# Layer 0 of a gated cross-attention kernel: stacks of two heads with the mask's rows in the contraction, loaded from DRAM, and row maxima taken bank by bank

## What is computed

```python
# layer 0: 16 heads of width 8; x is (16, 56, 128), ctx is (16, 1500, 128)
v = einsum('nlhd,od->nlho', ctx heads, Wv); k = ... Wk; q = einsum('nqhd,od->nqho', layernorm(x) heads, Wq)
energy = einsum('nqhd,nkhd->nhqk', q, k)
energy = where(mask == 0, -1e20, energy)              # mask: (16, 1, 56, 1500), all ones in the inputs
attn = softmax(energy / sqrt(128), axis=3)
x = x + tanh(g_xattn[0]) * (einsum('nhqk,nkhd->nqhd', attn, v).reshape(...) @ Wo.T + bo)
# then a routed feed-forward block (layer 0), attention with 16 heads of width 64 and a quantised block (layer 1)
```

## Time and profile before

| | us |
|---|---|
| median of 3 runs | 1247.57 |
| profiled execution | 1247.09 |
| its span, first to last instruction | 1245.3 |
| layer 0's attention, first row scores to the last block | 50 to 493 |
| TensorE busy over the span | 1132.1 |
| VectorE, ScalarE, GpSimd busy | 885.6, 699.6, 516.7 |
| mean granted TensorE clock | 0.972 |

### The profile page before, as it was taken

The page is one execution under the profiler, slowest core; times in us unless marked ns, Lnnn a source line. Parts: engine busy times, 40 slices in busy tenths (PEclk is TensorE's granted clock), DMA queues, the critical chain, the costliest instruction groups (busy, mean ns, idle before and its releaser), DMA issues.

```text
span 1245.3 us, 27942 instructions
## 1 busy us (share of the span) xinstructions
PE 1132.1 (91%) x10056; PEld 646.7 (52%) x10056; DVE 885.6 (71%) x1242; ACT 699.6 (56%) x967; POOL 516.7 (41%) x352
## 2 busy tenths in 40 slices
PE   4789999999999989778878999999999999999984
PEld 2255656566565646523434555555555555555542
DVE  7766666666666664587787868768676867867668
ACT  2345555555555536445566656666565656666542
POOL 8546666676666744332212322322232223223210
PEclk9899999999999989799998999999999999999996
DMA  3456565455554462000006776667575775667530
GB/s 106 123 169 199 167 182 156 150 156 159 179 157 151 133 157 66 1 1 26 1 13 131 145 143 135 144 136 151 123 145 117 147 149 126 147 133 150 112 63 15
DMA packets 222263, 151.29 MB, mean 121 GB/s; under 512 B 184576, under 2 KB 195312, under 8 KB 222208
## 3 DMA queue, kind: packets, MB, share of 16 engines
q1 hardware_dynamic: 221920, 150.56, 50.1%
q10 hardware_dynamic: 288, 0.00, 0.0%
HBM read 62.23 MB, written 25.39 MB: 70 GB/s over the span
## 4 chain that ended last, share of the span: by engine, by line
PE 75%; DVE 10%; issue 7%; ACT 6%; SPq 1%; DMA 1%; POOL 0%; ACTq 0%; DVEq 0%; POOLq 0%
PE bank L879 17%; PE bank L897 16%; PE bank L754 7%; PE bank L847 6%; PE bank L778 5%; PE bank L782 5%; PE bank L795 4%; DVE region L1701 2%; PE bank L855 2%; PE bank L919 2%; ACT region L1227 2%; PE bank L1120 2%; DVE e_row L1519 2%; PE bank L1082 1%; PE bank L825 1%
## 5 line engine op out<-in xcount | busy, mean ns | idle before, releaser
L1519 DVE CUSTOM_DVE_ANT_0 e_row<-bank,region 112x1500 f32<-112x1500 f32 x128 | 220.1, 1720 | 125.4 <-PE bank L754 124.1
L1227 ACT ACTIVATE region<-bank 125x896 f32<-125x896 f32 x192 | 176.0, 917 | 203.2 <-PE bank L782 203.2
L1558 DVE TENSOR_REDUCE neg_max<-bank 128x1 f32<-128x1500 f32 x112 | 192.7, 1721 | 130.7 <-PE bank L879 130.7
L879 PE MATMUL bank<-region 128*128 128x500 f16 x1008 | 235.1, 379 | 3.2 <-ACT e_row L1254 1.8
L1263 ACT COPY region<-bank 128x768 f16<-128x768 f16 x224 | 178.0, 794 | 88.2 <-PE bank L847 88.2
L1254 ACT ACTIVATE e_row<-bank,neg_shift 128x1500 f32<-128x1500 f32 x112 | 169.3, 1511 | 68.8 <-DVE neg_shift L1562 38.6
L573 POOL CAST u_w<-e_row 128x1500 f16<-128x1500 f32 x56 | 80.7, 1442 | 215.2 <-ACT e_row L1254 215.2
L573 POOL CAST wg_sb<-e_row 128x1500 f16<-128x1500 f32 x56 | 82.0, 1464 | 198.5 <-ACT e_row L1254 154.4
L879 PEld LDWEIGHTS bank<-region 128*128 (+1 forms) x1008 | 97.2, 98 | 107.9 <-issue 3.4
L778 PE MATMUL bank<-row_of,region 112*128 112x448 bf16 x384 | 137.7, 359 | 7.6 <-ACT region L1227 7.6
L782 PE MATMUL bank<-region 97*128 (+1 forms) x768 | 137.6, 260 | 0.0
(11 more groups left out here) (218 smaller groups left out, 1518.3 us busy)
## 6 DMA issues: line engine op xcount, KB each, us to landing
region<-region SPq DMA_DIRECT2D x192, 96.0 KB, 2.2
turned_rows<-region SPq DMA_DIRECT2D x16, 768.0 KB, 3.8
region<-turned_rows SPq DMA_DIRECT2D x32, 384.0 KB, 3.5
c_in<-in_ctx SPq DMA_DIRECT2D x16, 750.0 KB
split_rows<-region SPq DMA_DIRECT2D x16, 750.0 KB
region<-in_mask_Bx1xSxS_if SPq DMA_DIRECT2D x32, 328.1 KB
region<-split_rows SPq DMA_DIRECT2D x24, 250.0 KB
g_w<-split_rows SPq DMA_DIRECT2D x24, 250.0 KB
```

Of the source, the lines that this page charges most:

```text
L879: last = pe.matmul(score_banks1(par, t)[:, k, :], q1[:, ql, b, 128 * t:128 * (t + 1)], c_t1[par][:, cl, 4 * k:4 * k + 4, 0:KP], start=(ql ...
L1227: act.activation(p0[:, 2 * i:2 * i + 2, :], ring0("s", h, i)[0:KP, :, 0:HALF_ROWS], ACT.Exp, scale=SCALE0)\
L1519: dve.tensor_tensor_reduce(out=masked.rearrange("p (a k) -> p a k", a=3), in0=bank[0:R0, 0:3, 0:4 * KP], in1=mask_bias[par][:].rearrange(" ...
L1558: dve.tensor_reduce(neg_max[:, t:t + 1], score_banks1(par, t), AX.XY, ALU.max, negate=True)\
```

## The change

Layer 0 is rewritten as follows.

- **Stack.** A stack now holds two heads (one tile): rows 0 to 15 the high part, 16 to 31 the low, 32 the maximum, 33 to 48 the high again, and 49 to 104 the mask's 56 rows. There are 8 of them in a batch (HP), so KS = 105 rows.
- **Loads.** The stacks of batch b + 1 are loaded in `layer0(b)` in two halves of four. Each half has three DMAs from `turned_rows` in DRAM (16 rows x 4 stacks x 3 KB) and one that repeats the mask's rows four times (56 rows x 4 x 3 KB, within SBUF). They wait until `turned_out` of that batch has landed. Splitting, turning and storing are done two batches ahead, the transposes in h = 1 at i = 1 and 3.
- **Transposed scores.** A chunk is four matmuls of 112 columns with the four stacks; the mask's own matmul is gone.
- **Row maxima.** Each of a tile's three banks is reduced by itself, and each of its three matmuls waits for the reduction of that bank one tile earlier. One more small reduction a half combines them. The mask is in the scores already.
- **Places.** `c_split0` and `c_t0` move into the buffers of `g_w` and `u_w`; these weights are now loaded in batch 14 and both scaled by GpSimd in batch 15. The mask is read once in a batch, not twice. The preparation of q0 (64 rows instead of 96) is shorter by a few VectorE instructions.

```diff
 # places
-        c_stack = [carve([97, G, KC, 128], F16) for _ in range(2)]
+        c_stack = [carve([KS, HP, KC, 128], F16) for _ in range(2)]
-        c_split0 = carve([128, KC, 2, G, 32], F16)
-        c_t0 = carve([128, 2, KC, 128], F16)
+        c_split0, c_t0 = (w[:].rearrange("p e i -> p (e i)")[:, 0:KC * 128].bitcast(F16) for w in (g_w, u_w))
...
 # order of the PSUM pairs
-        RING0 = [("s", 0, 0), ("prep", 0), ("s", 0, 1), ("spread", 0), ("s", 0, 2), ("prep", 1), ("s", 0, 3), ("s", 0, 4),
-                 ("s", 0, 5), ("neg", 0), ("s", 1, 0), ("s", 1, 1), ("spread", 1), ("s", 1, 2), ("s", 1, 3), ("s", 1, 4),
-                 ("s", 1, 5), ("neg", 1)]
+        RING0 = [("s", 0, 0), ("s", 0, 1), ("spread", 0), ("s", 0, 2), ("s", 0, 3), ("s", 0, 4), ("s", 0, 5), ("neg", 0),
+                 ("s", 1, 0), ("s", 1, 1), ("prep", 0), ("spread", 1), ("s", 1, 2), ("s", 1, 3), ("prep", 1),
+                 ("s", 1, 4), ("s", 1, 5), ("neg", 1)]
...
         def sync_stack(sp, b, par):
             wait_apart(sp, "sp", (sem("st0"), (b - 1) * (2 * NP)))
-            for n in range(2):
-                wait_apart(sp, "sp", (sem(f"ct_done0_{n}"), b + 1))
-                for g in range(G):
-                    for at in ((0, 64), (32,))[n]:
-                        sp.dma_start(c_stack[par][at:at + 32, g], c_t0[32 * g:32 * g + 32, n])\
-                            .then_inc(sem(f"stack{par}_{g}"), 16)
+            wait_apart(sp, "sp", (sem("turned_out0"), 16 * (b + 1)))
+            wait_apart(sp, "sp", (sem("mask_done"), b + 1))
+            for half in range(2):
+                pairs = slice(4 * half, 4 * half + 4)
+                turned = turned_rows[b].rearrange("(g p) n c k -> p n g (c k)", p=2 * D0)
+                for at, n in ((0, 0), (2 * D0, 1), (33, 0)):
+                    sp.dma_start(c_stack[par][at:at + 2 * D0, pairs].rearrange("p g c k -> p g (c k)"), turned[:, n, pairs])\
+                        .then_inc(sem(f"stack{par}_{half}"), 16)
+                sp.dma_start(c_stack[par][KS - S:KS, pairs], mask_rows[par].unsqueeze(1).broadcast_to((S, 4, KC, 128)))\
+                    .then_inc(sem(f"stack{par}_{half}"), 16)
...
 # SyncE, a batch
             def layer0(b, par, first, last):
+                ahead = B - b if isinstance(b, int) else B
+                if ahead > 1:
+                    sync_stack(sp, b + 1, 1 - par)
+                if ahead > 3:
+                    sync_load_mask(sp, b + 3)
+                if ahead > 2:
+                    sync_split_out(sp, b + 2)
+                    sync_turned_out(sp, b + 2)
+                if ahead > 3:
+                    sync_load_context(sp, b + 3, 1 - par)
...
 # GpSimd, a batch
             def layer0(b, par, first, last):
-                if not last:
-                    mask0(b + 1, 1 - par)
+                if not (isinstance(b, int) and b + 2 >= B):
+                    mask0(b + 2, par)
+                    split0(b + 2, par)
...
-                if isinstance(b, int) and b >= B - 2:
+                if last:
                     pool.wait_ge(sem("in_ffn0"), 16 * 5)
-                    w = (g_w, u_w)[b - (B - 2)]
-                    pool.tensor_scalar(w[:], w[:], W_SCALE, None, ALU.mult).then_inc(sem("gu_scaled"), 1)
+                    for w in (g_w, u_w):
+                        pool.tensor_scalar(w[:], w[:], W_SCALE, None, ALU.mult).then_inc(sem("gu_scaled"), 1)
...
         def pe_rows0(pe, b, par, t):
-            if t % 2 == 0:
-                pe.wait_ge(sem(f"stack{par}_{t // 2}"), per_use(b, par, 48))
-            wait(pe, sem("max_done0"), b * T0 + t)
+            if t % 4 == 0:
+                pe.wait_ge(sem(f"stack{par}_{t // 4}"), per_use(b, par, 64))
             for k in range(3):
-                last = pe.matmul(bank[:, k, 0:4 * KP], q0_flat[0:96, bass.ds(b * ROWS + R0 * t, 128)],
-                                 c_stack[par][0:96, t // 2, 4 * k:4 * k + 4, 0:KP], start=True, stop=True)
-            last.then_inc(sem("scores0"), 1)
+                wait(pe, sem("bank_max0"), 3 * (b * T0 + t - 1) + k + 1)
+                pe.matmul(bank[:, k, 0:4 * KP], q0_flat[0:KS, bass.ds(b * ROWS + R0 * t, 128)],
+                          c_stack[par][0:KS, t, 4 * k:4 * k + 4, 0:KP], start=True, stop=True).then_inc(sem("scores0"), 1)
...
 # pe_st0
             for n in range(2):
                 c = 2 * i + n
-                into = ring0("s", h, i)[:, n, :]
-                pe.matmul(into[:, 0:HALF_ROWS], mask_flat[par][:, KP * c:KP * c + 128], row_of[:].rearrange("p h s -> p (h s)"),
-                          start=True, stop=False)
-                for g in range(2):
-                    rows = HALF_ROWS * h + GC * g
-                    last = pe.matmul(into[:, GC * g:GC * (g + 1)], c_stack[par][0:97, 2 * h + g, c, :],
-                                     q0[0:97, b, rows:rows + GC], start=False, stop=(g == 1))
+                for g in range(4):
+                    rows = HALF_ROWS * h + R0 * g
+                    last = pe.matmul(ring0("s", h, i)[:, n, R0 * g:R0 * (g + 1)], c_stack[par][0:KS, 4 * h + g, c, :],
+                                     q0[0:KS, b, rows:rows + R0], start=True, stop=True)
             last.then_inc(sem("st0"), 1)
...
         def dve_max0(dve, b, par, t):
-            if t == 0:
-                dve.wait_ge(sem("mask_done"), b + 1)
-            wait_apart(dve, "dve", (sem("scores0"), b * T0 + t + 1))
-            dve.tensor_tensor_reduce(out=masked.rearrange("p (a k) -> p a k", a=3),
-                                     in0=bank[0:R0, 0:3, 0:4 * KP],
-                                     in1=mask_bias[par][:].rearrange("p (a c) k -> p a (c k)", a=3),
-                                     scale=-1.0, scalar=3.0e38, op0=ALU.add, op1=ALU.min,
-                                     accum_out=neg_max[0:R0, t:t + 1]).then_inc(sem("max_done0"), 1)
+            for k in range(3):
+                dve.wait_ge(sem("scores0"), 3 * (b * T0 + t) + (k + 1))
+                dve.tensor_reduce(bank_max[0:R0, t, k:k + 1], bank[0:R0, k, 0:4 * KP], AX.X, ALU.max)\
+                    .then_inc(sem("bank_max0"), 1)
```

More of the change, by code:

```diff
@@ L517, in _ @@
             sync_split_out(sp, 0)
+            sync_turned_out(sp, 0)
             sync_stack(sp, 0, 0)
-            sync_turned_out(sp, 0)
             sync_load_mask(sp, 1)
-            batches(sp, layer0)
+            sync_split_out(sp, 1)
+            sync_load_context(sp, 2, 0)
+            sync_load_mask(sp, 2)
+            sync_turned_out(sp, 1)
+            layer0(0, 0, True, False)
+            layer0(1, 1, False, False)
+            with sp.Fori(1, LAST - 1) as i:
+                layer0(i * 2, 0, False, False)
+                layer0(i * 2 + 1, 1, False, False)
+            for b in range(B - 4, B):
+                layer0(b, b % 2, False, b == B - 1)
             sp.wait_ge(sem("split_out0"), 16 * B)
@@ L629, in mask0 @@
             def mask0(b, par):
-                wait_apart(pool, "pool", (sem("mask_in"), (b + 1) * 32), (sem("max_done0"), (b - 1) * T0),
-                           (sem("st0"), (b - 1) * (2 * NP)))
-                pool.tensor_scalar(mask_bias[par][:], mask_in[:].rearrange("q (p c) -> q c p", c=KC),
-                                   0.0, NEG, ALU.is_equal, ALU.mult).then_inc(sem("mask_done"), 1)
+                wait_apart(pool, "pool", (sem("mask_in"), 16 * (b + 1)))
+                if not (isinstance(b, int) and b < 2):
+                    for half in range(2):
+                        wait_apart(pool, "pool", (sem(f"stack{par}_{half}"), per_use(b - 2, par, 64)))
+                pool.tensor_scalar(mask_rows[par][:, :, 0:KP], mask_in.rearrange("q (p c) -> q c p", c=KC),
+                                   0.0, -MASK_ROW, ALU.is_equal, ALU.mult).then_inc(sem("mask_done"), 1)
             def context_pv0(b, par):
@@ L963, in layer0 @@
                                 pe_rows0(pe, after[0], after[1], 4 * after[2] + 2)
-                            if h == 0 and not last:
-                                wait_ring0(pe, b, par, "prep", 1)
-                                pe_prep0(pe, b + 1, 1, ring0("prep", 1))
                     if has_after:
@@ L1277, in act_context0 @@
                 act.wait_ge(sem("turned_out0"), 16 * b)
-                for g in range(G):
-                    act.wait_ge(sem(f"stack{1 - par}_{g}"), per_use(b - 1, 1 - par, 48))
             act.copy(c_t0[:, n].rearrange("p c k -> p (c k)"),
@@ L1312, in layer0 @@
                         act_exp0(act, b, par, h, i)
-                        if h == 0 and i in (0, 2) and not last:
-                            act_context0(act, b + 1, 1 - par, i // 2, ring0("prep", i // 2))
+                        if h == 1 and i in (1, 3) and not (isinstance(b, int) and b + 2 >= B):
+                            act_context0(act, b + 2, par, i // 2, ring0("prep", i // 2))
                         if h == 0 and i == 1 and par == 1 and not (isinstance(b, int) and b < 3):
```

(2 more changed lines are left out.)

163 lines of the change are left out of this document (81 added, 82 removed).

## The result

The changed kernel takes 1405.28 us (median of 4 runs, 1403.69 to 1406.92) against 1248.09: 1.126 times as long, interval 1.123 to 1.128. Slower was forecast, but by 37 us, not 157, and 1405 lies outside the stated range and above every rival. The profiled execution took 1403.69 us.

A forecast was written before the change was run, and what follows sets the result against it. The DMA queue, through five engines, was taken to bound the changed kernel at 29.0 us a batch instead of 26.1: +47 by batch 13, -14 for the last batches, +4 tail, total +37, 1285 us; 8-in-10 range 1198 to 1312.

The forecast's parts named there:

- The stall of about 5.6 us a batch: TensorE's wait for the stack before tile 0's row scores; about 5.6 us a batch, not shortening the DMA queue.
- a sum over five engines, 29.0 us: DMA queue per batch: 15.3 us without stacks, 9.8 for 16-row transfers, 3.9 for the mask; 29.0 us together.
- The clock: TensorE's clock may fall to 1.2 GHz after each stall; counted as nothing.
- rival 3: DMA queue with mask copies at 6.6 us: 31.7 us a batch, 1317 us; shares chance 0.60 with the forecast.
- TensorE's saving: Transposed scores: four 112-column matmuls start 0.05 us apart, a chunk takes 0.20 for 0.38 us, saving 4.3 us a batch.
- Rival 4: Transposed scores: small matmuls cost more than 0.05 us, at most 0.093; 1250 us with stacks hidden; chance 0.03.
- the 23.4 worked out: Engines alone, without the DMA queue: 21.8 + 1.0 + 0.6 = 23.4 us a batch.
- VectorE: Row maxima: a 500-column reduction takes 0.68 us, three about 1.85; VectorE's batch 19.5 us, under TensorE's 21.8.
- Start: First batches: second half of batch 0 starts at about 86 instead of 77 us, that of batch 1 12 us late.
- Tail: End of layer 0: ScalarE's first split casts wait for both weight scalings, one behind the other in batch 15; +4 us.
- All three DMA rivals: DMA queue per batch: stacks hidden 22.1 us, in between 26.8 us, worse than forecast 31.7 us.
- the hidden one: Stack loads stay hidden, 16-row transfers at the engines' rate: queue 22.1 us a batch, total 1197 us; chance 0.22.

The follow-up runs named there:

- Kernel 1: Changed kernel with the context's load issued ahead of the turned context's store: 1355.99 us, ratio 1.084.
- 7: Changed kernel with transposes in h = 0, GpSimd's split ahead of its mask, each stack half loaded after its last reader: 1486.57 us.
- Kernel 5: Changed kernel with the 125-row context load and split context store each moved as 112 and 13 rows: 1291.67 us, ratio 1.032.
- Kernel 10: Changed kernel with stacks loaded for batches 0 and 1 only, GpSimd's mask behind the second division in two instructions, its load behind the context's: 1221.96 us.
- kernel 3: Changed kernel with stacks loaded for batches 0 and 1 only: 1249.97 us, ratio 1.002.
- kernel 6: Changed kernel with the context's load ahead of the turned context's store, and 125 rows moved as 112 and 13: 1274.65 us, ratio 1.019.
- kernel 9: Changed kernel; 112 and 13 rows, transposes in h = 0, stack halves loaded behind context and mask, GpSimd's mask in two pieces, scaling by expert: 1242.25 us.
- kernel 12: Kernel before the change with maxima bank by bank, 112 and 13 rows, and weights' scaling by expert: 1234.15 us, ratio 0.989.

## Why the prediction was wrong

**The step that failed** is "The stall of about 5.6 us a batch doesn't shorten the queue: the next split goes out when its context has come in, the next turned context after it, and the stack behind both", and with it the batch as a sum over five engines, 29.0 us. It took the queue as always full and TensorE as what waits for it. But the queue waits for TensorE too: stack, h = 1, transposes, store, stack. What counts is the sum of latencies around that loop, 37.3 us. Kernels 1 and 7 change the order of the work alone, not a byte and not an engine, and give 33.7 and 43.9 us a batch for 37.3, which no sum of bytes per engine explains. Kernel 5 takes the load off the five, and still waits for its stacks. The parts were all to be seen: the order of the issues in the diff, TensorE's half of 12.4 us, and the context's load ahead of the stack. I even wrote the chain down for the start, and not for the steady part.

**The clock: a term put at nothing.** The prediction says of TensorE's lower level "it has the slack, so I count nothing". But TensorE's half with the transposes is a term of the loop. Kernel 10 has the same stretch, from the row scores to the turned context's store, without a stall before it:

```profile
254.95:265.65 10.70, 10.03 (x174) 6.68 (x174) 7.96 (x13) 6.67 (x8) 10.46 (x9) 1.00 0.19 72
```

10.7 us at a granted clock of 1.00, against 13.1 at 0.78 in the changed kernel, whose clock is at 0.50 (1.2 GHz) for the first 5.4 us behind the wait. That is 2.4 us a turn, some 31 of the 144 us.

**Sizes.** By the packets in the trace the queue is in flight 34 of 37.3 us, not 29. The context's load holds the five engines 13 us beside the stack's writes, where I took the 5.9 of the earlier trace rows; what they have of the stack and mask behind it takes 11, not 13.7; nothing is in flight for 3.3, not 0. The rate to 16 rows was right, the one to the mask's was not. Kernel 1's queue with stack alone, then with mask rows alone:

```profile
317.00:321.00 4.00, 0.92 (x16) 0.59 (x12) 1.39 (x4) 1.35 (x3) 4.00 (x4) 1.00 1.05 128
321.50:324.50 3.00, 0.00 (x0) 0.00 (x0) 0.00 (x0) 0.00 (x0) 1.90 (x3) 0.50 1.01 208
```

128 GB/s to 16 rows (forecast 120), 208 to the mask's 56, whose upper bound of 6.6 us holds and not the 3.9 that I took. With these rates the five engines' sum is 15.3 + 9.2 + 6.6 = 31.1 us, close to rival 3's 31.7, and still 6 short of the batch. The Trainium skill (SBUF — State Buffer, Door 1: The DMA port swizzle) gives 109 for four ports; the trace has a sixth more, in a window in which three transfers to different groups of 16 rows follow one another.

**TensorE's saving: right.** Eight matmuls of 112 columns take 0.57 us at full clock, and one lasts 0.224 on average:

```profile
319.37 0.57 PE L797 MATMUL bank<-region 105*128 x8 [0.27 <-ACT u_w L1295]
```

They start (0.57 - 0.224) / 7 = 0.05 apart. Rival 4 is out. The Trainium skill (TensorE: Matmul & The Clock Gate, Back-to-back issue gap) has 81 ns at 128 columns; this trace does not agree. Kernel 10 has 23.7 us a batch against the 23.4 worked out.

**VectorE.** Reductions last 672 ns and three take 1.85 us, as said. Missed: GpSimd's mask, which before began once TensorE's last scores were through, has lost that wait and comes to lie beside the negation once no stack is waited for, worth 2 us a batch (kernel 3 against 10). In the changed kernel itself it costs little: TensorE waits 9.6 us in 100 to 440 us for negations.

**Start: right for batch 0 only.** The second half of batch 0 began at 87.66, forecast about 86. That of batch 1 was forecast 12 us late: the negation ahead of it is (115.64 for 103.56), but its row scores wait 8.3 us more for the stack and come at 124.33 for 104.22, 20 us late. The loop already holds there. **Tail: right.** Forecast +4, measured +5.6: both scalings stand in a row ahead of ScalarE's casts (timeline of TensorE, GpSimd and ScalarE, answering).

```profile
87.66 1.43 PE L774 MATMUL bank<-region 105*128 105x500 f16 x3 [12.37 <-DMA region<-e_row]
...
124.33 1.43 PE L774 MATMUL bank<-region 105*128 105x500 f16 x3 [8.33 <-DMA region<-region]
...
631.53 6.08 POOL L706 TENSOR_SCALAR g_w<-g_w 128x2304 f32<-128x2304 f32 x1
637.56 6.06 POOL L706 TENSOR_SCALAR u_w<-u_w 128x2304 f32<-128x2304 f32 x1
...
643.65 0.83 ACT L1340 CAST region<-g_w 128x768 f16<-128x768 f32 x1 [4.35 <-POOL u_w L706]
647.67 0.35 ACT L1258 ACTIVATE block_t<-bank,bo_col 128x112 f32<-128x112 f32 x1 [0.99 <-PE bank L829]
```

**The rivals.** All three DMA rivals were sums of the same kind. Even the hidden one, 1197 us, is refuted: with no stack loaded behind the first two (kernel 3) the change gives 1250, and with the mask out of the way too (kernel 10) 1222.

## What to carry to other kernels

When a change makes a transfer read what another has just written, look for the loop that it closes: list, for one turn, store, landing, load, landing, the compute up to the next store. Its latencies add, whatever the engines' shares are, and the place of every unrelated DMA in the queue is one of its terms. Only when no such loop is longer than the batch does the sum of bytes per engine decide. And a transfer of 125 rows is worth cutting into 112 and 13 as soon as someone waits for it.

## What was not expected of the hardware

- 125 rows run on five engines at 131 GB/s, 112 and 13 rows at 356 (kernel 6). The Trainium skill (DMA: Bandwidth & Descriptors, Why a DMA increments its semaphore by 16 and not by 1) has the rule: as many engines, up to 16, as divide the slowest dimension evenly, so 5 for 125, 16 for 112, 13 for 13. The traces agree for 125 (a share of 0.32) and for 112 with 13 (0.98); none shows the 13 alone. I had used the five engines in the sum and not asked what another cut would give.
- A 6 KB packet on the five engines takes 0.8 to 1.0 us while the others write 3 KB pieces to 16 rows, about 0.5 while they write the mask's 56 rows, 0.23 alone. Why stays open.
- VectorE's instruction on one to four columns takes up to 4.7 us beside GpSimd instructions that work in SBUF (4.73, 2.57 in kernel 3, 3.2 in kernel 9), while its reductions from PSUM beside the same ones keep their 0.67, three in 1.85 us. The Trainium skill (GPSIMD Engine Reference, Key points) says that the two contend when a VectorE instruction has two inputs in SBUF, which these have and the reductions don't; the traces agree. The scaling in nine pieces, 7.4 us in all, took the wait of 4.73 us away (kernel 12). In kernel 9 the 3.2 us lie beside whole instructions that follow one another.
